# A landmark-attention and expert layer on one NeuronCore: the query stage with three expert banks, one denominator row per head, and a shifted query side

## The reference

```python
Phi_Q = jnp.exp(-C_Q / temperature)          # squared distances of Q to the landmarks
Phi_K = jnp.exp(-C_K / temperature)
Z = jnp.einsum('bhnk,bhnd->bhkd', Phi_K, V)
Y = jnp.linalg.solve(W_kernel, Z)
out_unnorm = jnp.einsum('bhnk,bhkd->bhnd', Phi_Q, Y)
norm = jnp.maximum(Phi_Q @ solve(W_kernel, sum of Phi_K), 1e-10)   # one number per row and head
out = (out_unnorm / norm) @ Wo.T + bo
x = layernorm(x + out)
gate_logits = x @ Wg.T + bg                  # 8 experts, the best two, softmax of the two
ffn = sum over the two of gate_w * (x @ We[e].T + be[e])
x = layernorm(x + ffn)
```

## Time and profile before

| | |
|---|---|
| median of 3 runs | 2029.69 us (2024.14 to 2030.82) |
| the profiled execution: its own time, its span | 2032.55 us, 2030.8 us |
| granted TensorE clock, mean over the span | 0.952 of full speed |
| busy, share of the span | PE 89%, DVE 76%, ACT 60%, POOL 46% |
| first bias product of the query stage | at 687.2 us |
| last one | at 1996.2 us |

### The profile page before, as it was taken

The page is one execution under the profiler, slowest core; times in us unless marked ns, Lnnn a source line. Parts: engine busy times, 40 slices in busy tenths (PEclk is TensorE's granted clock), DMA queues, the critical chain, the costliest instruction groups (busy, mean ns, idle before and its releaser), DMA issues.

```text
span 2030.8 us, 42773 instructions
## 1 busy us (share of the span) xinstructions
PE 1811.0 (89%) x16312; PEld 1369.3 (67%) x16312; DVE 1534.3 (76%) x3316; ACT 1225.9 (60%) x2411; POOL 931.6 (46%) x1179
## 2 busy tenths in 40 slices
PE   4668999989884899999999999999999999999997
PEld 3267778878772676676667767667676667766765
DVE  5668854888434788888888888887888878888874
ACT  2246665766655466568557566655855756675553
POOL 2300000000001376666666677656766666666666
PEclk8689999999996899999999999999999999999999
DMA  2586696766955233333243333333324333333300
GB/s 81 78 179 144 159 199 142 179 160 166 196 146 142 68 82 96 89 90 88 73 109 93 80 94 78 96 87 94 89 73 105 87 91 90 77 86 92 89 27 21
DMA packets 210753, 214.02 MB, mean 105 GB/s; under 512 B 59228, under 2 KB 142580, under 8 KB 210292
## 3 DMA queue, kind: packets, MB, share of 16 engines
q1 hardware_dynamic: 210356, 210.75, 43.0%
q0 software_dynamic: 192, 0.52, 0.1%
HBM read 61.26 MB, written 23.59 MB: 42 GB/s over the span
## 4 chain that ended last, share of the span: by engine, by line
PE 42%; DVE 26%; POOL 12%; issue 10%; SPq 5%; DMA 3%; ACT 2%; DVEq 0%; POOLq 0%; ACTq 0%
PE bank L299 9%; PE bank L300 9%; PE bank L301 9%; POOL x_tok L549 3%; PE bank L1606 3%; PE bank L1496 3%; PE bank L1636 2%; POOL part_x L562 2%; POOL part_x L561 2%; DVE phi L1177 2%; PE bank L1512 2%; DVE nrm L1199 2%; PE bank L1497 2%; DVE if L1256 2%; DVE inversion L1053 2%
## 5 line engine op out<-in xcount | busy, mean ns | idle before, releaser
L299 PE MATMUL bank<-weh,x1h 128*128 128x512 f32 x1024 | 433.3, 423 | 36.8 <-DVE y_out L1299 17.6
L300 PE MATMUL bank<-weh,x1l 128*128 128x512 f32 x1024 | 408.9, 399 | 0.0
L301 PE MATMUL bank<-wel,x1h 128*128 128x512 f32 x1024 | 408.6, 399 | 0.0
L549 POOL TENSOR_TENSOR x_tok<-x_tok,bo_sb 128x1024 f32<-128x1024 f32 x32 | 76.8, 2401 | 531.7 <-DMA x_tok<-in_x 531.7
L841 ACT ACTIVATE part_x<-bank,gate 128x256 f32<-128x256 f32 x512 | 211.3, 477 | 171.0 <-PE bank L301 166.9
L299 PEld LDWEIGHTS bank<-weh,x1h 128*128 128x128 f32 x1024 | 195.2, 191 | 156.3 <-issue 60.5
L786 ACT ACTIVATE phi<-bank,nlt_cur,invt 128x512 f32<-128x512 f32 x256 | 187.0, 793 | 86.5 <-PE bank L1606 86.5
L301 PEld LDWEIGHTS bank<-wel,x1h 128*128 128x128 f32 x1024 | 195.3, 191 | 47.8
L641 ACT ACTIVATE phi<-bank,invt 128x512 f32<-128x512 f32 x256 | 162.6, 684 | 105.2 <-PE bank L1497 105.0
L300 PEld LDWEIGHTS bank<-weh,x1l 128*128 128x128 f32 x1024 | 195.9, 191 | 34.2
L561 POOL TENSOR_TENSOR part_x<-part_x 128x512 f32<-128x512 f32 x128 | 177.8, 1389 | 32.6 <-ACT part L841 32.4
(11 more groups left out here) (198 smaller groups left out, 4465.5 us busy)
## 6 DMA issues: line engine op xcount, KB each, us to landing
x_raw<-in_xT SPq DMA_DIRECT2D x64, 512.0 KB, 4.4
q_stack<-kh SPq DMA_DIRECT2D x256, 128.0 KB, 2.4
x_tok<-in_x SPq DMA_DIRECT2D x32, 512.0 KB, 3.9
q_stack<-kl SPq DMA_DIRECT2D x128, 128.0 KB, 2.4
q_stack<-key_aug SPq DMA_DIRECT2D x128, 128.0 KB, 2.5
k_hl<-attn_h SPq DMA_DIRECT2D x32, 256.0 KB
k_ha<-attn_h SPq DMA_DIRECT2D x32, 256.0 KB
k_hl<-attn_l SPq DMA_DIRECT2D x32, 256.0 KB
```

Source lines behind the costliest of these rows:

```text
L299: nc.tensor.matmul(outp, ah, bh, start=first, stop=False)
L300: nc.tensor.matmul(outp, al, bh, start=False, stop=False)
L301: return nc.tensor.matmul(outp, ah, bl, start=False, stop=last)
```

## The change

The query stage is rewritten in its order, and in four of its parts.

1. Expert products rotate over three banks (2, 3, 5). DVE takes products 0 and 2 of a tile, ACT 1 and 3. POOL makes two additions per tile instead of three.
2. The denominators are made once per head and row: 32 narrow matmuls into 128 x 128 of bank 1. DVE clamps and inverts 128 columns, once per chunk. The inverses are stored to DRAM (`den_dram`), and two DMAs read them back, each row repeated for the 16 channels of its head, into `attn`. DVE then multiplies in place.
3. The gate logits are made transposed, as 16 matmuls with 32 output rows, saved by ACT and turned back by one transpose. The gates need one transpose instead of four, and the bias product two matmuls instead of four.
4. The query side is shifted earlier: the distances 0 to 3 of chunk q + 1 are made at the end of the turn, the query projection before the attention of q, and the landmarks have two buffers. The copies of Z and of the norms are gone.

```diff
+        def expert_bank(p, n):
+            return bank[(2, 3, 5)[(16 * p + n) % 3]]
...
+            def store_inverses(c):
+                sp.wait_ge(inv_ready, c + 1)
+                sp.wait_ge(inv_spread, SPREAD * c)
+                sp.dma_start(den_dram.rearrange("h t n -> t h n"), den_inv[:]).then_inc(inv_stored, 16)
+            def spread_inverses(c):
+                sp.wait_ge(attnl_ready, 2 * c)
+                sp.wait_ge(inv_stored, 16 * (c + 1))
+                for s in range(KC):
+                    heads = den_dram[HPS * s:HPS * s + HPS].rearrange("h t n -> h (t n)")
+                    sp.dma_start(attn[:, s], rep(heads, 1, HD)).then_inc(inv_spread, 16)
...
             def sum_parts(p, t):
-                own.then(nc.gpsimd.tensor_tensor(a[0], a[0], a[2], ALU.add))
...
-                own.then(V.tensor_scalar(nrm[:], bank[at + 1][:], NORM_MIN, None, ALU.max))
-                own.did(V.reciprocal(nrm[:, 0:CH // 2], nrm[:, 0:CH // 2]))
...
+            def invert_denominators(c):
+                dve.wait_ge(den_done, c + 1)
+                dve.wait_ge(inv_spread, SPREAD * c)
+                V.tensor_scalar(den_inv[:], bank[1][:, 0:P], NORM_MIN, None, ALU.max).then_inc(den_read, 1)
+                dve.wait_ge(den_read, c + 1)
+                V.reciprocal(den_inv[:], den_inv[:]).then_inc(inv_ready, 1)
+            def normalise(c, s, at=4):
+                dve.wait_ge(out_done, 2 * c + s + 1)
+                dve.wait_ge(inv_spread, SPREAD * (c + 1))
+                V.tensor_tensor(attn[:, s], bank[at][:], attn[:, s], ALU.mult).then_inc(attn_ready, 1)
...
+            def denominators(c):
+                pe.wait_ge(qphi_ready, PAIRS * (c + 1))
+                pe.wait_ge(h_done, TPC * (c + 1))
+                for i in range(PAIRS):
+                    for t in range(TPC):
+                        last = mm(bank[1][32 * t:32 * t + 32, 0:P], y_cur[:, i, 32:64], phi[:, i, t * P:(t + 1) * P],
+                                  start=(i == 0), stop=(i == PAIRS - 1))
...
-                for n, dst in ((0, bank[at]), (32, bank[at + 1])):
...
+                for k in range(KC):
+                    for u, a in enumerate((x1h[at], x1l[at])):
+                        for t in range(TPC):
+                            last = mm(bank[0][32 * t:32 * t + 32, 0:P], wg_s[:, k], raw(a[:, k, t * P:(t + 1) * P]),
...
             def experts(p, n):
+                at, last_user = p % 2, 16 * p + n - 3
+                if last_user >= 0:
+                    pe.wait_ge((comb_done, part_ready)[last_user % 2], last_user // 2 + 1)
```

More of the change, by code:

```diff
@@ new lines, in _ @@
+            for p in range(NCH):
+                q = p + 2
+                if p % CPB == 0 and p // CPB + 1 < BATCH:
+                    sp.wait_ge(y_done, p // CPB + 1)
+                    load_inverse(p // CPB + 1)
+                if p:
+                    store(p - 1, 0)
+                load_rows(q)
+                stack_queries_hi(q + 1)
+                store_inverses(q)
+                stack_queries_lo(q + 1)
+                spread_inverses(q)
+                stack_query_norms(q + 1)
+                if p:
+                    store(p - 1, 1)
+                load_query_x(q + 3)
@@ L548, in residual @@
                 pool.wait_ge(xt_loaded, 16 * (c + 1))
-                nc.gpsimd.tensor_tensor(x_tok[:], x_tok[:], rep(bo_sb[:], 1, TPC), ALU.add).then_inc(xb_ready, 1)
+                for tp in range(2):
+                    two = x_tok[:, 2 * tp:2 * tp + 2]
+                    last = nc.gpsimd.tensor_tensor(two, two, rep(bo_sb[:], 1, 2), ALU.add)
+                last.then_inc(xb_ready, 1)
             def ln1(c):
@@ L941, in _ @@
+            result(NCH - 1, 2)
+            result(NCH - 1, 3)
         @block.vector
@@ L1393, in _ @@
+            finish(NCH - 1, 3)
         @block.tensor
@@ L1681, in gate_transposes @@
                 pe.wait_ge(gst_ready, p + 1)
-                for t in range(TPC):
-                    last = nc.tensor.transpose(bank[1][0:24, t * P:(t + 1) * P], g_st[:, t], ident)
-                last.then_inc(gtr_done, 1)
+                nc.tensor.transpose(bank[1][:, 0:P], g_st[:].rearrange("p t e -> p (t e)"), ident).then_inc(gtr_done, 1)
             def bias_term(p):
@@ L1794, in _ @@
-            for b in range(BATCH - 1):
-                turn(b)
-            turn(BATCH - 1)
+            pe.wait_ge(attn_ready, 4)
+            for p in range(NCH):
+                c, q = p + 1, p + 2
+                nxt = c % 2
+                experts(p, 0)
+                query_dists(q, range(4, 6))
+                experts(p, 1)
+                output_projection(c)
+                query_dists(q, range(6, 8))
+                experts(p, 2)
+                experts(p, 3)
+                queries(q + 1, 1)
+                denominators(q)
+                experts(p, 4)
+                attention(q, 0)
+                experts(p, 5)
+                query_norms(q + 1)
+                experts(p, 6)
+                x1_transposes(c, nxt)
+                experts(p, 7)
+                experts(p, 8)
+                gate_logits(c, nxt)
+                experts(p, 9)
+                logit_transpose(c)
+                experts(p, 10)
+                attention(q, 1)
+                experts(p, 11)
+                query_dists(q + 1, range(0, 2))
+                experts(p, 12)
+                experts(p, 13)
+                query_dists(q + 1, range(2, 4))
+                if begins_batch(q + 1):
+                    z_transposes((q + 1) // CPB)
+                experts(p, 14)
+                gate_transposes(c)
+                experts(p, 15)
+                bias_term(c)
+                if begins_batch(q + 1):
+                    landmark_solve((q + 1) // CPB)
```

590 lines of the change are left out of this document (274 added, 316 removed).

## The result

The changed kernel takes **2075.76 us** (median of 4 runs, 2063.62 to 2080.21) against 2029.47 for the kernel before in the same comparison: a ratio of 1.0224, 95% interval 1.0176 to 1.0271. It is 2.2% slower. The forecast was 1967 us, 3.1% faster, with 0.07 on slower.

What follows compares the result with a forecast made beforehand. TensorE was taken as the bound. Per turn 38.7 work + 0.3 gates + 0.3 trip + 0.5 new batch + 0.1 clock = 39.9 us against 42.2, saving 71; start +9, end -1: 1967 us, 8-in-10 range 1925 to 2012.

Steps and rivals of the forecast that it cites:

- TensorE's work: TensorE's work per query-stage turn: -0.5 us (bounds -0.95 and -0.2), leaving 38.7; denominators 2.3, from the query norms' row.
- The other engines: VectorE about 3 us a turn less, ScalarE 8 weighings and GpSimd 4 additions less; none the bound, none counted.
- The banks: Expert products over three banks: the waits on y_out and y_spare counted as gone, 1.0 us a turn.
- The gates: TensorE's wait before the gate transpose: 0.3 us a turn, bounds 0 and 1.8.
- New batch: Landmark work on ACT: 1.3 us at logits, 1.1 at first distances, in 7 of 31 turns; 0.5 a turn.
- The trip through DRAM: Inverses' store and two reads: landed at 27.0, hidden with nothing to spare; 0.3 us a turn added, bounds 0 and 1.
- the prediction's clock: Time in us within a turn, with 0 at the start of the turn's experts 0.
- the slower rival: Trip's reads land late, TensorE waits at the gate transpose; landing at 30.0 gives 2085 us; chance 0.07.
- A wait of the multiplication on the reads of over 3 us: Sign at VectorE's multiplication by the inverses: such a wait would make the prediction wrong.
- Clock: TensorE's lower clock follows its waits; with these mostly gone, 0.1 of 0.8 us a turn left.
- Start: Ahead of turn 0 nothing hides the trip of chunks 0 and 1: +9 us, bounds 4 and 12.
- an end: End of the kernel: one POOL addition less, 1 us won.

Runs made afterwards that it cites:

- L: Changed kernel with both multiplications later on VectorE, second attention half behind experts 12, ScalarE's and GpSimd's splits behind them: 2091.2 us with 8-wide reads, 1997.66 with wide reads.
- N: Changed kernel with the next chunk's norms issued ahead of the reads on SP: 2128.28 us; together with L, 8-wide reads: 2009.66 us; with L and wide reads: 2006.08.
- the doubled store: Changed kernel with the inverses stored twice side by side in DRAM, so reads start from 16 rows with the right values: 1997.89 us, 0.9864.

## Why the prediction was wrong, step by step

**TensorE's work** was right. A turn of 43.1 us less 3.65 idle and 68.2 / 2 / 31 = 1.1 of clock leaves 38.4, forecast 38.7. The denominators take 1.88 us to the start of the next product (1331.85 to 1333.73) and not 2.3: the row of the norms was too dear, and the lower bound, 1.86, was nearer.

**The other engines**: the reciprocal takes 0.95 us (forecast 0.9), the clamp 0.28 (0.3). VectorE's work fell by (1077.4 - 906.7) / 31 = 5.5 us a turn and not 3; the forecast counted nothing on it.

**The banks**: the waits went as forecast. The term gave the third bank 31 x 1.0 us; without the trip the bank is worth 6. With two banks 19 of the 31.5 us of waits were there again, but in part in the place of others.

**The gates**: 13.4 us, 0.4 a turn, forecast 0.3. Of the held instructions that spoke for more, the cast has a median of 0.17 us now. A wait as large was not in the sum: 13.7 us of L302 on L1327, before the output projection, until VectorE has added the bias.

**New batch**: at the logits TensorE waited for x1 for 9.1 us in 7 batch turns, 1.3 each, as forecast. Of the 1.1 us at the first distances the kernel without the trip shows 0.2. So the term was 0.3 us a turn and not 0.5.

**The trip through DRAM** is the step that failed, "hidden with nothing to spare". It failed three times over.
- The size: each read was priced at 2.7 us, the landing of a result's store with as many bytes. The distance was 7.0 us. The same bytes 16 wide took 4.2, and 8 wide with the norms out of the way 5.2. A store that starts from 128 partitions was no model for two reads in flight that start from 8 rows, with four more DMAs behind them, and the count of bytes hid this. The 2.6 us that the prediction estimates by the Trainium skill, "DMA: Bandwidth & Descriptors", Anatomy of one DMA, missed it in the same way; that section's figures are of DMAs that GpSimd issues, these are SP's, and the measurement decides. The late landing puts the end of the trip 12.3 us after the inverses, not 8.6, so at 18.4 + 12.3 = 30.7 on the prediction's clock, past the 30.0 for which the slower rival gave 2085 us. It was 2076. What spoke against this rival, that the trip would have to take half as long again, is what happened, and 0.07 was too little for a term with no row of its shape. A wait of the multiplication on the reads of over 3 us was named as a sign of being wrong: it was 4.7.
- The place: I had each late us show at the gate transpose. It showed at the second attention half, which needs bank 4 from the same multiplication, 71 us, and the gate transposes behind it did not wait longer. I had read the multiplication's consumers on VectorE's list only, not by the bank that it frees.
- The other consumer: three more instructions on SP were counted for their time, not for who stands behind them. The norms of the next chunk do. Whichever of the two consumers was relieved alone, the other kept the time at 2085 to 2128 us (8-wide reads). Relieving both gave 2010.

**Clock**: 1.1 us a turn and not 0.1. The stage has 68 us at the lower level with the trip and 5 without it. That the lower clock follows TensorE's waits was too simple, though: the kernel with wide reads and bank 5 for the second half idles 79 us in the stage, more than the 69 of the kernel before, and has 5 us at the lower level where that has 51.

**Start**: +19 us against +9. Without the trip the first bias product is at 701.0, still 14 later than before, so most of it is the order, and 5 us are the trip. The distances of chunk 2 now come ahead of the first bias product and wait for their stack. The trace of the changed kernel and that of the kernel without the trip have this wait at

```profile
699.43 1.22 PE L1643 MATMUL bank<-q_stack,l_stack 128*128 128x512 f32 x2 [15.26 <-DMA q_stack<-key_aug]
```

```profile
694.25 1.22 PE L1639 MATMUL bank<-q_stack,l_stack 128*128 128x512 f32 x2 [8.25 <-DMA q_stack<-key_aug]
```

The prediction named this dependence and put no number of its own on it.

The forecast of 1967 us and the 1965 of the kernel without the trip agree, partly by luck: the turn was right (39.9 against 39.8), and a start 5 us dearer than forecast was made up by the stage, which saved 76 us and not 71, and by an end 1.5 us cheaper than forecast. The 1965 also leave out any price of the division, for which the forecast had 0.3 us a turn.

**What stays open**: why the hidden trip still leaves some 7 us beside the waits that the view names, and whether a place exists in which bank 4, the combining and the reads all fit. Spreading the inverses on TensorE, with no DMA, wasn't tried on the chip.

## What to carry to other kernels

Price a DMA by a row of the same shape on its outermost dimension, not of the same bytes; if the trace has none, the range must reach far. When something is late, list all who need it: the instruction that waits, the bank or buffer that it frees, and what stands behind it on its queue. Relieving one of two late consumers gained nothing here, and could have looked like a refutation; the trial that counts relieves both. And take the suspect out altogether first: one kernel without the trip told what everything else of the change was worth.

## What the runs showed of the hardware

- Two reads of 256 KB each, DRAM to SBUF, had landed 6.9 us after the second's issue when they started from 8 rows and 4.1 us from 16 rows, with the same bytes, the same 2 KB per partition and four DMAs of 128 KB right behind them. With these four ahead of them the 8-wide reads took 5.1. Reading 128 different rows in groups of 8 x 16 took 7.3, with the four behind.
- Other DMAs land later right behind the reads. These are the landings (KB each, median us) in the changed kernel, then with L and N, where the norms go out ahead of the reads; without any reads it is 2.6, right behind wide ones 4.1. Ahead of wide reads, in the kernel with L, N and the doubled store, it is 3.7, so the order is not all of it:

```profile
q_stack<-key_aug SPq DMA_DIRECT2D x128, 128.0 KB, 5.5
```

```profile
q_stack<-key_aug SPq DMA_DIRECT2D x128, 128.0 KB, 2.7
```

- The cast of the choice of experts, 1103 ns in the median before, had a median of 172 ns in the changed kernel with four GpSimd additions a turn fewer. Whether these are the reason was not tried. Another small instruction, the last multiplication of the gates, has a median of 164 ns there and 1008 ns in the kernel without the trip, with the same additions.

```profile
L1298 DVE CAST if<-i x32: 170/172/1224, 702.4 to 2037.0; 128x8 f32<-128x8 uint32 x32
```
